# Second layer of a mixture of experts in split parts for three of every four chunks, in a four-stage transformer kernel

## The reference

```python
logits = x @ Wr + br; route_w = softmax(logits)
mask = one_hot(top_k(route_w, 2)).sum(-2)
routed = route_w * mask; routed /= routed.sum(-1)
h = relu(einsum('bsd,edh->ebsh', x, W1) + b1)        # 8 experts, 128 -> 512
expert_out = einsum('ebsh,ehd->ebsd', h, W2) + b2    # 512 -> 128
out = einsum('bse,ebsd->bsd', routed, expert_out)
```

```python
scores = x @ w_router; top_idx = top_k(scores, 384)
out = x.at[batch, top_idx].set(gelu(x[top_idx] @ w_block))
```

## Time and profile before

| | |
|---|---|
| median of 3 runs | 1470.9 us (1470.77 to 1471.15) |
| the profiled execution | 1468.7 us, span 1466.6 us |
| TensorE busy | 1403.2 us, 96% of the span |
| VectorE busy | 1059.6 us, 72% |
| ScalarE busy | 1098.1 us, 75% |
| GpSimd busy | 851.9 us, 58% |
| mean granted clock of TensorE | 0.981 |

### The profile page before, as it was taken

How to read it: one execution, slowest core, us unless ns; L and a number is a source line. 1 busy time by engine, 2 the same in 40 slices (tenths; PEclk the granted TensorE clock), 3 DMA queues, 4 the chain that set the end, 5 groups by cost and what they waited for, 6 DMA issues and landing times.

```text
span 1466.6 us, 17689 instructions
## 1 busy us (share of the span) xinstructions
PE 1403.2 (96%) x6304; PEld 718.6 (49%) x6304; DVE 1059.6 (72%) x1944; ACT 1098.1 (75%) x943; POOL 851.9 (58%) x667
## 2 busy tenths in 40 slices
PE   6999999999999999999999999699999999999974
PEld 3433434434433443443444343256777777777753
DVE  6786777777777777777777677654677687786674
ACT  2799789879978978978878879845676676676741
POOL 4568767777777678768867876721333333333320
PEclk9999999999999999999999999899999999999985
DMA  3001111011001002001101103333011011010100
GB/s 114 0 16 23 30 30 24 15 45 23 16 16 51 16 16 51 16 17 30 37 16 30 30 16 96 89 123 103 0 66 58 8 66 55 11 66 8 59 7 8
DMA packets 45847, 55.09 MB, mean 38 GB/s; under 512 B 13825, under 2 KB 32513, under 8 KB 44609
## 3 DMA queue, kind: packets, MB, share of 16 engines
q1 hardware_dynamic: 45760, 53.97, 12.3%
HBM read 49.11 MB, written 4.85 MB: 37 GB/s over the span
## 4 chain that ended last, share of the span: by engine, by line
PE 89%; DVE 7%; POOL 1%; ACT 1%; issue 1%; DMA 0%; SPq 0%; DVEq 0%; POOLq 0%
PE sc L383 16%; PE av L396 14%; PE pj L74 13%; PE z L74 12%; PE y L1095 8%; PE sc L378 6%; PE y L74 5%; PE pj L362 4%; PE pj L412 4%; PE pj L404 2%; DVE w L541 2%; PE tb L1026 1%; POOL wsum L303 1%; PE tb L1040 1%; PE tb L1053 1%
## 5 line engine op out<-in xcount | busy, mean ns | idle before, releaser
L541 DVE TENSOR_SCALAR w<-sc 128x1024 f32<-128x1024 f32 x256 | 301.3, 1218 | 117.3 <-PE sc L383 115.2
L632 ACT ACTIVATE w<-w 128x2048 f32<-128x2048 f32 x128 | 237.5, 1904 | 144.5 <-DVE w L541 144.2
L303 POOL TENSOR_TENSOR wsum<-wsum,w 128x512 f32<-128x512 f32 x256 | 329.0, 1285 | 20.1
L882 POOL TENSOR_TENSOR hr_l<-hr,hr_h 128x512 fp32r<-128x512 f32 x112 | 150.2, 1341 | 265.0 <-ACT hr L928 265.0
L383 PE MATMUL sc<-query,key 64*128 64x512 f32 x1024 | 254.4, 615 | 0.0
L396 PE MATMUL av<-w,vt 128*64 128x512 f32 x1024 | 237.6, 607 | 6.4 <-DVE gT L548 5.2
L636 ACT ACTIVATE w<-w 128x2048 f32<-128x2048 f32 x128 | 240.2, 1901 | 0.4
L640 ACT ACTIVATE w<-w 128x2048 f32<-128x2048 f32 x128 | 239.6, 1895 | 0.0
L928 ACT ACTIVATE hr<-z,b 128x512 f32<-128x512 f32 x256 | 173.7, 684 | 77.3 <-PE z L74 77.2
L289 POOL TENSOR_TENSOR sqq<-query 128x512 f32<-128x512 f32 x64 | 66.5, 1040 | 223.0 <-DVE query L495 220.9
L300 POOL TENSOR_TENSOR wsum<-w 128x512 f32<-128x512 f32 x128 | 164.5, 1285 | 11.5 <-ACT w L640 11.5
(11 more groups left out here) (183 smaller groups left out, 2237.6 us busy)
## 6 DMA issues: line engine op xcount, KB each, us to landing
hT<-head_recips SPq DMA_DIRECT2D x64, 256.0 KB, 4.0
rb<-routing SPq DMA_DIRECT2D x8, 2048.0 KB, 7.0
w<-in_W SPq DMA_DIRECT2D x16, 256.0 KB, 5.0
xa<-in_X SPq DMA_DIRECT2D x8, 256.0 KB, 4.4
xc<-in_X SPq DMA_DIRECT2D x8, 256.0 KB, 2.8
x<-xc SPq DMA_DIRECT2D x8, 256.0 KB, 4.0
out<-prod SPq DMA_DIRECT2D x8, 256.0 KB, 2.3
x<-x SPq DMA_DIRECT2D x1, 1792.0 KB, 10.9
```

The source lines that it names most:

```text
L303: nc.gpsimd.tensor_tensor(wsum[:, u, :], wsum[:, u, :], w[:, j % 2, u, c, :], ALU.add).then_inc(s_added, 1)
L541: nc.vector.tensor_scalar(w[:, s, 2 * r:2 * r + 2, c, :], sc[:, i, :, :], 0.0, None, ALU.max).then_inc(s_d2, 1)
L632: nc.scalar.activation(w[:, j % 2, u, :, :], w[:, j % 2, u, :, :], ACT.Sqrt).then_inc(s_sqrt, 1)
```

## The change

Three things change. First, `in_parts(n)` becomes true for chunks 1, 2 and 3 of each expert from batch 1 on, instead of 1 and 3: 168 chunks by parts where there were 112. `part(n)` numbers them, the parts of hr get 5 buffers each in place of 3, and `split_w2` makes parts of three chunks of an expert's second-layer weights, in steps 25 to 32 instead of 24 to 31. TensorE waits for an expert's parts when it first needs them in batch 1, not for all at the head of batch 1. Second, `w1` is freed once split; the low parts of w2 take 12 KB of its place and `scr` the other 4 KB. Third, `scr` therefore has one place for all four c, so each pair of instructions in `token_ranks` is now followed by a `link`.

```diff
-        w1 = sb("w1", [P, NE, FF])
+        with ExitStack() as until_split:
+            w1 = until_split.enter_context(nc.sbuf_tensor("w1", [P, NE, FF], F32))
+        w2_l = sb("w2_l", [P, NE * (NF - 1), D], F32R)
+        scr = sb("scr", [P, 2, T])
...
-        w2s = [sb("w2_h", [P, NE * NF // 2, D], F32R), sb("w2_l", [P, NE * NF // 2, D], F32R)]
-        hrs = [sb("hr_h", [P, HR // 2, T], F32R), sb("hr_l", [P, HR // 2, T], F32R)]
+        w2s = [sb("w2_h", [P, NE * (NF - 1), D], F32R), w2_l]
+        HP = 5
+        hrs = [sb("hr_h", [P, HP, T], F32R), sb("hr_l", [P, HP, T], F32R)]
...
-        N_T = 13
+        N_T = 16
...
         def in_parts(n):
-            return n >= NU and n % 2 == 1
+            return n >= NU and n % NF > 0
+
+        def part(n):
+            return n // NF * (NF - 1) + n % NF - 1
...
-            for n in range(NU + 1, B * NU, 2):
-                m = n // 2
-                pool.wait_ge(S["hr"], n + 1)
-                nc.gpsimd.tensor_tensor(hrs[1][:, m % (HR // 2), :], hr[:, n % HR, :],
-                                        hrs[0][:, m % (HR // 2), :].bitcast(F32), ALU.subtract).then_inc(S["lo"], 1)
+            for n in range(NU, B * NU):
+                if in_parts(n):
+                    pool.wait_ge(S["hr"], n + 1)
+                    nc.gpsimd.tensor_tensor(hrs[1][:, part(n) % HP, :], hr[:, n % HR, :],
+                                            hrs[0][:, part(n) % HP, :].bitcast(F32), ALU.subtract).then_inc(S["lo"], 1)
...
-                    pe.wait_ge(S["lo"], (n - NU) // 2 + 1)
-                    m = product(nc, y[:, g % 2, :], [w[:, k // 2, :] for w in w2s],
-                                [v[:, n // 2 % (HR // 2), :] for v in hrs], start=False, stop=(i == NF - 1))
+                    if b == 1 and i == 1:
+                        pe.wait_ge(S["w2s"], 2 * (NF - 1) * (k // NF + 1))
+                    pe.wait_ge(S["lo"], part(n) - part(NU + 1) + 1)
+                    m = product(nc, y[:, g % 2, :], [w[:, part(k), :] for w in w2s],
+                                [v[:, part(n) % HP, :] for v in hrs], start=False, stop=(i == NF - 1))
...
-                    pe.wait_ge(S["w2s"], NE * NF)
...
-                if c == NC - 1:
-                    lt(t, ins)
+                lt(t, ins)
...
-                chunks = slice(NF // 2 * e, NF // 2 * (e + 1))
-                source = w2[:, NF * e + 1:NF * (e + 1):2, :]
+                parts = slice((NF - 1) * e, (NF - 1) * (e + 1))
+                source = w2[:, NF * e + 1:NF * (e + 1), :]
...
-                if b == 0 and k >= 24:
-                    if k == 24:
+                if 25 <= n < 25 + NE:
+                    if n == 25:
                         dve.wait_ge(att["x1_out"], 16 * B)
-                    dve.wait_ge(in_w2[k - 24], 16)
-                    split_w2(k - 24)
+                    dve.wait_ge(in_w2[n - 25], 16)
+                    split_w2(n - 25)
```

More of the change, by code:

```diff
@@ L763, in build_rest @@
         score = sb("score", [P, NC])
-        scr = w1[:, :, :].rearrange("p (i c) t -> p i c t", i=2)
         above = sb("above", [P, 2, NC])
         keep = sb("keep", [P, 2, NC])
-        w2s = [sb("w2_h", [P, NE * NF // 2, D], F32R), sb("w2_l", [P, NE * NF // 2, D], F32R)]
-        hrs = [sb("hr_h", [P, HR // 2, T], F32R), sb("hr_l", [P, HR // 2, T], F32R)]
+        w2s = [sb("w2_h", [P, NE * (NF - 1), D], F32R), w2_l]
+        HP = 5
+        hrs = [sb("hr_h", [P, HP, T], F32R), sb("hr_l", [P, HP, T], F32R)]
         gel, res = o1, prod
@@ L925, in hidden @@
                 if in_parts(n):
-                    nc.scalar.activation(hrs[0][:, n // 2 % (HR // 2), :], z[:, n % 2, :], ACT.Relu,
+                    nc.scalar.activation(hrs[0][:, part(n) % HP, :], z[:, n % 2, :], ACT.Relu,
                                          bias=b1[:, n % NU:n % NU + 1])
@@ L1281, in token_ranks @@
                 dve.wait_ge(S["score_ps"], t + 1)
-                V.tensor_scalar(scr[:, 0, c, :], tb[:, 1, :], score[:, c:c + 1], None, ALU.is_gt, ALU.add, accum_out=above[:, 0, c:c + 1])
-                ins = V.scalar_tensor_tensor(scr[:, 1, c, :], tb[:, 1, :], score[:, c:c + 1],
+                V.tensor_scalar(scr[:, 0, :], tb[:, 1, :], score[:, c:c + 1], None, ALU.is_gt, ALU.add, accum_out=above[:, 0, c:c + 1])
+                ins = V.scalar_tensor_tensor(scr[:, 1, :], tb[:, 1, :], score[:, c:c + 1],
                                              ttri[:, (NC - 1 - c) * P:(2 * NC - 1 - c) * P], ALU.is_equal, ALU.mult,
                                              accum_out=above[:, 1, c:c + 1])
-                if c == NC - 1:
-                    lt(t, ins)
+                lt(t, ins)
             def kept(t):
@@ L1313, in split_w2 @@
             def split_w2(e):
-                chunks = slice(NF // 2 * e, NF // 2 * (e + 1))
-                source = w2[:, NF * e + 1:NF * (e + 1):2, :]
[L1316 to L1319, removed]
+                parts = slice((NF - 1) * e, (NF - 1) * (e + 1))
+                source = w2[:, NF * e + 1:NF * (e + 1), :]
+                V.tensor_copy(w2s[0][:, parts, :], source).then_inc(S["w2s"], NF - 1)
+                dve.wait_ge(S["w2s"], (NF - 1) * (2 * e + 1))
+                V.tensor_tensor(w2s[1][:, parts, :], source, w2s[0][:, parts, :].bitcast(F32),
+                                ALU.subtract).then_inc(S["w2s"], NF - 1)
             def weigh(g):
```

## The result

The kernel after the change takes **1479.0 us** (median of 5 runs, 1477.1 to 1480.6), the kernel before 1470.9 (5 runs, 1469.4 to 1471.5). The ratio is 1.0056 with an interval of 1.0042 to 1.0071: slower by 8.1 us, 6.2 to 10.4. Forecast were 1477.1, the range 1471.5 to 1481.5, and "slower" with 0.68. The profiled execution took 1480.4, its span is 1478.6, 12.0 above the span of before.

The account below looks back on a forecast made before the run. It took TensorE's queue to bound the expert batches. Saving -8.9, roots +9.75, gelu +1.0, collision +3.6 and links with last batch +0.8 sum to +6.25, giving 1477.1 us; range 1471.5 to 1481.5.

Parts of the forecast that it names:

- Saving: TensorE's second-layer products: each by parts instead of plain saves 0.165 us, 54 times, -8.9 us.
- The roots: Square roots' table loads on ScalarE: one more relu (hr_h) stalls TensorE's z 0.75 us more at 13 places, +9.75 us.
- Gelu: Behind ScalarE's gelu: chunk 6's hr_h makes z of chunk 8 stall TensorE 0.17 us in batches 2 to 7, +1.0.
- The collision: Denominators' multiply on VectorE held by GpSimd's subtraction for chunk 23: o1's transposes stall 0.6 us in batches 1 to 6, +3.6.
- GpSimd and the rest of VectorE: GpSimd's 8 more subtractions a batch against VectorE: only the denominators' place priced, +3.6 us; GpSimd's own queue no matter.
- The last batch: Last batch: GpSimd's chunk 30 pushes chunk 31 by about +0.1 us.
- Links: Link after each pair in token_ranks: three more of 0.12 us, on the path twice in the tail, +0.7 us.
- splits: Splits of second-layer weights grow by half, covered by VectorE's 4.22 us idle behind them: nothing added.
- TensorE's moved wait: TensorE's wait for an expert's weight parts, moved to first need in batch 1: covered, nothing added.
- The rival without a collision: Denominators' multiply starts ahead of GpSimd's subtraction, so no hold there: +2.65 in all, 1473.5 us; chance 0.28.
- ScalarE's cover: ScalarE's 17 idle us a batch absorb the extra relus, the 13 stalls stay at 0.1: 1462.8 us; chance 0.12.
- Late VectorE: At the root, statistics come 0.3 us after the table load; with a second hit at add_weighed +4, 1481 us; chance 0.14.

Follow-up runs that it names:

- e4: Kernel after, but parts of hr made for odd chunks only, chunk 2 of an expert multiplying chunk 1's parts: saved products alone; 1464.3 us, ratio 0.9963.
- e7: Kernel after with the first square root of a batch, and its table load, before plain chunk 12 instead of 11; 1475.5 us, ratio 1.0033.
- e9: Kernel after with both roots before plain chunks, scores' transposes, their copy and token_ranks later, denominators' last multiply by columns; 1480.9 us, ratio 1.0074.
- e12: Kernel after without the denominators' last multiply, both roots before plain chunks, scores and token_ranks later, half the result writes behind the norm; 1463.0 us, ratio 0.995.
- e8: Kernel before with only the link after each pair of token_ranks added; 1469.7 us in one execution.
- e1: Kernel after with chunks 10 and 30 of a batch, right before the two square roots, plain again; 1473.1 us, ratio 1.0024.

## Why the prediction was right, and by how much it was off

- **Saving, 0.165 a product.** Right: 1.21 us over 7 products of a batch, 0.17 each; alone in e4.
- **The roots, +0.75 at 13 places.** Right: 0.77, 13 waits, seen in after, gone at the first root in e7 by the move of its load alone, at the second in e9 and at both in e12, there with other moves beside. ScalarE's 17 idle us a batch didn't help, since they lie elsewhere than behind the table load.
- **Gelu, +0.17.** Right: z 8 is at 0.00 where e4, without the relu, has -0.18.
- **The collision, +0.6 in 6 batches.** Right, 0.72, by the sequence that was stepped.
- **GpSimd and the rest of VectorE: mis-sized.** The sum has the collision at the denominators and no other stall on GpSimd's account. The step that failed is that I stepped VectorE only up to the transposes of o1. Past them L1217, L1345 and L1225 are held, where before it was L1210 and L1219, and the transposes of the routing wait 0.29: 6 x 0.29 = 1.7 us.
- **The last batch, "+0.1": mis-sized.** About 0.8 (0.77 between the same operations of VectorE in the two traces). The prediction has GpSimd's chunk 30 push chunk 31 there, and nothing for VectorE; its norm multiplies were held by 1.7, of which the next operation gave 0.95 back.
- **Links +0.7, splits 0, TensorE's moved wait 0.** Right: 0.76 in e8, and no wait for the weight parts in after.

With the two sizes mended the sum is 6.25 + 1.7 + 0.7 = 8.7; the traces have 8.9 from z of chunk 32 on, and the medians 8.1. That these lie so close is in part luck: the collision is 0.7 us and the roots 0.3 above their terms, the saving 0.4 larger than its own, and small places take off 0.5. The rival without a collision fell at its own margin, 0.10 us. That ScalarE's cover is there after all is excluded by z 1 and z 13 at 0.77 each; the one at z 13 vanishes in e7 with the place of the load alone. Late VectorE did not happen in the kernel after, with 0.18 us to spare; it did in e1, by 0.16, and in e9.

Open is why the opening's loads land a microsecond later in some executions, and whether all of the 3.2 us follow from it: no kernel was made for it.

## What to carry to other kernels

When the bounding engine works through a ring of two buffers, an idle share of the engine that empties it says little: sum what stands between two of its releases (a table load and two long operations here) against the bounding engine's own work there, and remember that a saving just before such a place is given back. An operation that GpSimd gets must be laid against each VectorE operation whose result is due soon, on to the next place where the bounding engine waits for VectorE, not only to the first. In e12 both table loads before plain chunks, the scores and ranks a little later, two small operations fewer in the denominators and half of the result writes behind the statistics turned +8 us into -6.5.

## What was unexpected of the hardware

GpSimd's hold does not ask for size or for two tensors: operations of 32 columns took 0.83 (L1205, L1225) where one took 0.19 unheld, 16 columns of a TENSOR_SCALAR 1.24, and GpSimd's own subtraction, 1.29 alone, went up to 1.83 (at 1245.93, with VectorE's L1281 started 0.01 before it):

```profile
L890 POOL TENSOR_TENSOR hr_l<-hr,hr_h x168: 1263/1289/1830, 1020.2 to 1422.8; 128x512 fp32r<-128x512 f32 x168
```

(durations in ns: shortest, median, longest). And single executions of the same opening code lay up to 3.7 us apart by z of chunk 32, more than most steps of this study, so a single profile's span is no measure of a change of this size; distances from batch to batch are: those of batches 2 to 6 in the kernel after are 1.22 to 1.27 us above before.
